# Attention and two mixture-of-experts layers on one core: two places in which four groups of value matmuls are issued

## The reference, cut to what matters

```python
q = (query @ Wq + bq)          # query = seq2 + b_self
k = (key @ Wk + bk)            # key = [seq1 + b_prev, seq2 + b_self]
v = (value @ Wv + bv)
score_prev = einsum('bhqd,bhkd->bhqk', q, k[:, :, :l1]) * SCALE
score_self = (q * k[:, :, l1:]).sum(-1, keepdims=True) * SCALE
weights = softmax(concatenate([where(mask, score_prev, -inf), score_self], -1))
attn = einsum('bhqk,bhkd->bhqd', weights[..., :-1], v[:, :, :l1]) + weights[..., -1:] * v[:, :, l1:]
return attn @ Wo + bo
```

## Time and profile before

| what | us or share |
|---|---|
| runs | 511.44, 518.4, 517.86 (median 517.86) |
| profiled execution, its own time | 516.34 |
| its span, first to last instruction | 514.6 |
| mean granted TensorE clock | 0.925 |
| TensorE matmul busy | 433.5 us, 84% |
| VectorE busy | 290.3 us, 56% |
| ScalarE busy | 243.9 us, 47% |
| GpSimd busy | 226.3 us, 44% |
| scores, L768 | 128 records, 70.7 us |
| transposes, L780 | 256 records, 48.8 us |
| values, L793 | 512 records, 27.4 us |

### The profile page before, as it was taken

One profiled execution on the slowest core, in us unless ns is written; L12 is line 12 of the kernel. 1 busy time (PEld: TensorE's weight loads), 2 busy tenths in 40 slices (PEclk: granted clock), 3 DMA queues, 4 the chain that ended last, 5 costly groups with the idle time before them and its releaser, 6 DMA issues.

```text
span 514.6 us, 11629 instructions
## 1 busy us (share of the span) xinstructions
PE 433.5 (84%) x2768; PEld 295.8 (57%) x2769; DVE 290.3 (56%) x1209; ACT 243.9 (47%) x751; POOL 226.3 (44%) x260
## 2 busy tenths in 40 slices
PE   3699989999999997799999999887582899898840
PEld 2355546565555644399898987356531467676630
DVE  2568898778878888423333332255362436576534
ACT  1277757777777774155454553245230123343310
POOL 3347783344333343524444443545566003555540
PEclk9999999999999998879999999878577799999985
DMA  2007999888889999656666660401111201222207
GB/s 60 10 13 178 255 244 244 215 229 216 222 213 246 242 237 314 190 167 178 174 172 178 173 180 22 163 0 37 38 47 47 52 1 37 67 77 70 62 16 242
DMA packets 58373, 71.10 MB, mean 138 GB/s; under 512 B 8754, under 2 KB 34599, under 8 KB 58208
## 3 DMA queue, kind: packets, MB, share of 16 engines
q1 hardware_dynamic: 52752, 60.89, 45.1%
q0 software_dynamic: 4736, 8.47, 5.1%
q10 hardware_dynamic: 848, 1.32, 0.9%
HBM read 35.58 MB, written 36.37 MB: 140 GB/s over the span
## 4 chain that ended last, share of the span: by engine, by line
PE 59%; DVE 15%; issue 8%; DMA 5%; ACT 5%; another core or an unknown queue 3%; POOL 3%; SPq 2%; ACTq 1%; POOLq 0%; DVEq 0%
PE bank L915 9%; PE bank L909 8%; PE bank L768 7%; PE bank L1079 5%; PE bank L780 5%; DVE mx L1413 3%; PE bank L1095 2%; PE bank L793 2%; DVE ps L1420 2%; PE bank L1005 2%; PE bank L1006 2%; PE bank L1016 2%; PE bank L1094 2%; ACT ps L1131 1%
## 5 line engine op out<-in xcount | busy, mean ns | idle before, releaser
L1226 ACT ACTIVATE hT<-bank,w 128x128 f32<-128x128 f32 x176 | 51.0, 368 | 56.0 <-PE bank L909 40.0
L768 PE MATMUL bank<-qexp 128*128 128x512 f32 x128 | 70.7, 635 | 0.8 <-POOL qexp L677 0.8
L698 POOL DMA_INDIRECT expert_outputs<-yb,idr x44 | 43.2, 983 | 57.8 <-DVE yb L1586 40.7
L686 POOL DMA_INDIRECT expert_rows<-rows,slots x32 | 31.5, 986 | 83.7 <-DVE slots L1436 76.6
L748 POOL DMA_INDIRECT layer_outputs<-w_all,idr x40 | 39.3, 983 | 63.5 <-DVE w_all L1785 48.3
L780 PEld LDWEIGHTS bank<-ident,ps 128*128 128x128 f32 x256 | 33.0, 142 | 54.0 <-ACT ps L1137 26.0
L1137 ACT ACTIVATE ps<-bank,ntop 128x128 f32<-128x128 f32 x192 | 54.8, 378 | 7.6 <-DVE ntop L1416 7.6
L780 PE MATMUL bank<-ident,ps 128*128 128x128 f32 x256 | 48.8, 295 | 5.7 <-ACT ps L1131 2.7
L915 PE MATMUL bank<-w_all,hT 128*128 x352 | 50.3, 287 | 2.5 <-ACT hT L1226 1.6
L1146 ACT ACTIVATE pT<-bank 128x512 f32<-128x512 f32 x64 | 38.2, 597 | 28.7 <-PE bank L780 26.5
L1413 DVE TENSOR_REDUCE mx<-bank 128x4 f32<-128x512 f32 x64 | 44.0, 687 | 13.7 <-PE bank L768 8.7
(11 more groups left out here) (294 smaller groups left out, 897.9 us busy)
## 6 DMA issues: line engine op xcount, KB each, us to landing
expert_rows<-fill SPq DMA_DIRECT2D x64, 390.0 KB, 6.0
w<-in_L_ffn_w_dram SPq DMA_DIRECT2D x40, 258.0 KB
w_all<-in_L_ffn_w_dram SPq DMA_DIRECT2D x24, 256.0 KB
xt<-expert_rows SPq DMA_DIRECT2D x45, 65.0 KB
w_all<-expert_rows SPq DMA_DIRECT2D x40, 65.0 KB, 1.2
qexp<-layer_outputs SPq DMA_DIRECT2D x4, 512.0 KB, 5.7
aux<-in_L_ffn_b_dram SPq DMA_DIRECT2D x1, 1536.0 KB
qexp<-expert_outputs SPq DMA_DIRECT2D x3, 512.0 KB, 3.8
```

The lines of the kernel that those rows point to most:

```text
L698: g.indirect_dma_start(ys_dram, bass.IndirectOffsetOnAxis(ap=idr[r][:, 0:1], axis=0), yb[r][:, :], None, bounds_check=YS1 - 1, oob_is_err= ...
L768: pe.matmul(psA[j % 2][:, :], qexp[p][:, j, :], kexp[p].rearrange("p g k -> p (g k)"), start=True, stop=True).then_inc(a_in_ps, 1)
L1226: s.activation(hT[r % 2][:, c, :], banks[c][:, 0:P], ACT.Gelu, bias=w1[r][:, F0 + c:F0 + c + 1]).then_inc(gelu_done, 1)
```

## The change

The four calls of `weighted_values` in TensorE's step are moved; their number, operands and waits stay, and no other engine's program changes. The values of group 2 now come at the end of quarter 0, with those of group 3, which leave quarter 1. The values of group 0 come at the end of quarter 2, behind the middle matmuls and the wait for `prod_ready`, with those of group 1, which leave quarter 3. So the four groups of a batch are issued as two pairs.

```diff
                 scores(i, p, 0)
                 turned_weights(i, 3, 3)
-                weighted_values(i, 1 - p, 2, 3)
                 if active(i, 4):
...
                     pe.matmul(ps_v, xfT[1 - p][:, 0:P], wv[:, :], start=True, stop=True)
                     pe.matmul(ps_vs, xfT[1 - p][:, P:2 * P], wv[:, :], start=True, stop=True)
+                weighted_values(i, 1 - p, 2, 3)
+                weighted_values(i, 1 - p, 3, 3)
 
 
                 scores(i, p, 1)
                 turned_weights(i, 0, 2)
-                weighted_values(i, 1 - p, 3, 3)
                 if active(i, 1):
...
                 scores(i, p, 2)
                 turned_weights(i, 1, 2)
-                weighted_values(i, p, 0, 2)
                 if active(i, 1):
                     pe.wait_ge(prod_ready, i)
...
                 if m is not None:
                     m.then_inc(mid_in_ps, 1)
+                weighted_values(i, p, 0, 2)
+                weighted_values(i, p, 1, 2)
 
 
                 scores(i, p, 3)
                 turned_weights(i, 2, 2)
-                weighted_values(i, p, 1, 2)
                 if active(i, 0):
```

## The result

The changed kernel takes 519.68 us (median of 20 runs, 516.38 to 522.83); the kernel before, in 20 runs of the same comparison, 516.91 us (511.44 to 518.59). The ratio is 1.0062, 95% interval 1.004 to 1.0084: by this ratio 3.2 us slower (the two medians differ by 2.8), small but clear of noise, and within 2%. The profiled execution has a span of 518.6 us, 4.0 more than before.

The account below looks back on a forecast made before the run. The prediction took a loop through group 3's exponentials, VectorE's maxima, `prod` and group 2's transposes as the bound, not TensorE. Ten steps by 0.34 us gave 3.4; 516.34 + 3.4 = 519.7, say 520 us, range 511 to 526.

Parts of the forecast that it names:

- What bounds the kernel: A loop: group 3's exponentials, VectorE's maxima to `prod`, middle matmuls, scores 3, group 2's transposes, ScalarE's copy; TensorE has slack.
- Price of a group: On TensorE, a lone value group costs 0.48 us, a second right behind it 0.24, so a pair 0.72.
- Quarter 2: The pair behind the middle matmuls delays scores 3 by 0.72 us and group 2's last transpose by 0.34 in the mean.
- Quarter 3: Without group 1's values 0.48 us is gained before the next input, but the loop hangs on the last transpose.
- Quarter 0: The pair ahead of scores 1 delays them up to 0.47 us, absorbed by two existing waits; cost nothing.
- both covers: Waits hiding late scores 1: group 0's transposes for an exponential, VectorE's late taking of scores 1; without them up to 0.47 us per step.
- How many steps: No loss in the first five softmax steps; nine from 75.38 to 174.64 and the last lose 0.34 each, 3.4 us.
- Behind attention: The expert layer starts when the last rows are in DRAM, so the 3.4 us arrive there whole.
- The range: From below 511 us, called halfway from nothing moved to 508.6, to 526, with about 2 in 10 outside.
- TensorE's pace: Rival: TensorE sets the pace, each pair saves 0.24 us, twice for 16 batches: 7.7 us faster, 508.6; 13%.
- The clock: Rival: TensorE's idle ahead of the middle matmuls lowers its clock, 0.71 us in each of ten steps: 526.8 us; 10%.

Follow-up runs that it names:

- Group 1 late: Kernel before, with group 1's values moved from quarter 3 to behind scores 0 of the next step, nothing paired: 0.9894; repeated on the other chip: 0.9896.
- doubled gates: Kernel before, with the gate matmul at the end of quarter 3 issued twice: ratio 1.0053, eight steps 89.73 us.
- groups 0 and 1 alone: Kernel before, with only the values of groups 0 and 1 moved to the end of quarter 2 (quarters 2 and 3 change): ratio 0.9945.
- groups 2 and 3 alone: Kernel before, with only the values of groups 2 and 3 moved to the end of quarter 0: ratio 0.9947.

## Why the prediction was right, and where it was not

The number was right: 3.4 us slower forecast, 3.2 measured, 520 against 519.68. That it was so close was luck. The place of the loss was not the forecast one: from `prod` to the next scores 0, where 0.34 was to be lost per step, 0.25 was gained, and from scores 0 to `prod`, where nothing was to be lost, it was 0.41. The sum came out by errors of opposite sign. What was right is the first half of the mechanism: the value group that ran in the wait for `prod` now stands behind it, and the delay goes over ScalarE's copy to the exponentials of group 3. What failed is where it goes from there, and what quarters 0 and 3 do to it.

- *What bounds the kernel.* Half wrong. "VectorE starts its maxima at 132.12, having waited for them" took the named releaser for the cause. The maxima waited for scores 0 (1.24 us behind their start in the earlier trace rows, as in all eight steps). All that follows on quarter 3 and quarter 0 rests on this.
- *Price of a group.* Right. The second group follows the first by 0.24 us, and a pair's record is 0.65 long against 0.43. A pair adds 0.66 to 0.67 where it stands, forecast 0.72 (scores 3 behind the middle 1.21 instead of 0.55). The 0.20 us idle stays once per pair. The Trainium skill, "TensorEngine Tiling (Array Packing)", section Key Properties, has a change of tiling mode drain the engine, and this idle time agrees with it. What the pairs save by it was less than what their places cost.
- *Quarter 2.* Right in its place: scores 3 come 1.21 behind the middle, forecast 1.25 to 1.3, and TensorE stands idle ahead of it, 0.54 us for its matmuls and 0.73 for its weight loads, forecast nearly 1. The transposes run unpaced, as forecast. That this lengthens the step by 0.34 was wrong: from `prod` to scores 0 the steps got shorter.
- *Quarter 3.* Wrong: "the loss goes round the loop whole; the gain does not". Maxima 0 hang on scores 0, so the 0.5 us that group 1 left there were gained. Group 1 late shows it from one side (-0.3 per step; the repeat on the other chip is 0.5 below the kernel before on this one), the doubled gates from the other (+0.27). With quarters 2 and 3 alone the kernel is faster.
- *Quarter 0.* Wrong: "Cost: nothing". The bound for scores 1 held only if the exponentials of group 3 stayed where they were against scores 0; they start 0.56 behind them instead of 0.05 and now pace the transposes of group 3, so scores 1 come at 3.53 and 3.31 in turn instead of 2.47, and maxima 1 wait. The text priced each quarter with the others held still. "Were both covers gone, up to 0.47 per step" was nearest to what happened: with the changed quarters 0 and 1 it is 0.41 (7.87 instead of 7.46), and from groups 0 and 1 alone to the whole change (88.95 - 86.98) / 8 = 0.25 per step.
- *How many steps.* Forecast: none in the first five steps, 0.34 in each from 75.38 on. Measured: 0.17 per step in the eight (1.35, where 2.7 was expected), and 1.26 us ahead of them. Of the early steps the first got 0.69 shorter and the two at 39.51 and 51.33 together 1.88 longer (11.82 and 11.99 instead of 11.02 and 10.91). The transposes of group 0 start there 5.41 and 5.07 us behind scores 0 (3.97 and 3.78 before) and `prod` ends 3.30 behind them (3.29 before). The text took later exponentials of group 1 for harmless; in these steps `prod` hangs on them.
- *Behind attention.* Right: what is lost arrives at the first expert activation (2.66 us).
- *The range.* Its lower end, 511, is called halfway from 516.3 to 508.6; halfway is 512.5. The measured time is far from either.
- *The rivals.* TensorE's pace: refuted as a description of the whole, though half of it was true, since quarter 3 was on the loop. The clock: it did not fall in these steps (1.00). Even the fall of the step at 75.38 is absent (1.00 at 76.58), after a step with 11.13 busy of 13.26 us where it had been 10.98 of 13.37. That is not the change's merit: with group 1 late, the clock was 0.92 in the step at 75.13 of one execution and 1.00 at 75.09 in the repeat, there after 10.86 busy of 13.25 us. The Trainium skill, "TensorE: Matmul & The Clock Gate", section What's actually happening, has the clock follow how busy the array has been recently; these rows do not show what decided between fall and no fall.

## What to carry to other kernels

When several engines run in step, price a reordering around the whole loop and not quarter by quarter: here each half of the change gained 0.5% and both lost 0.6%, because they spent the same slack. A releaser named in a trace is a guess: check in another step, or in the code's wait, whether the waiting instruction could start without it. Doubling one cheap instruction in a stretch tells whether that stretch is on the loop: 0.22 us more cost 0.04, 0.23 and 0.27 us per step in three places. Put short independent work into a wait that exists (group 1 behind scores 0, 1.05% faster) before saving the cost of issuing it.

## What was not expected of the hardware

The program takes about 516.9 us on some chips and 486.9 on another, with nearly the same attention. In the same kernel (group 1 late) on the two, 25 of the 30 us lie in the second expert layer: its matmuls run from 367.64 to 491.66 on one and from 362.80 to 461.55 on the other.

A VectorE `ntop` of 128x4 elements takes 0.17 us mostly. When it falls on GpSimd's tensor work it ends with that work: 0.32 us in each of the eight steps (139.34, GpSimd's operation ending at 139.31), and 3.01 us from 69.77 to 72.78, while three GpSimd operations ran one behind the other until 72.75. In the kernel before, all 19 that take over 0.3 us end 0.02 to 0.04 us behind a GpSimd tensor operation. Small moves of TensorE's order make such a wait come or go: the step at 174.64 took 11.25 us before, 10.62 with the change and 10.23 with groups 2 and 3 alone.
